# Expert tiles in groups of four, their narrow down halves on two row groups of TensorE

## What is computed

```python
x = x + xattn(layernorm(x), ctx, ctx, Wh, wg_w, wo_w, gn_gamma, gn_beta)
h = layernorm(x)
scores = softmax(h @ gate_w.T)                       # 64 experts
topk_w, topk_ids = top_k(scores, 6); topk_w /= sum(topk_w)
# for each expert e and each of its rows:
gu = h @ w_gate_up[e].T                              # 176 gate, 176 up
routed += comb[:, e] * ((silu(gu[:176]) * gu[176:]) @ w_down[e].T)
sgu = h @ ws_gate_up.T                               # shared: 352 gate, 352 up
out = x + routed + (silu(sg) * su) @ ws_down.T
```

## Time and profile before

| | |
|---|---|
| time, median of 3 runs | 310.27 us (308.89 to 312.10) |
| the profiled execution | 307.54 us, of which 305.7 us are the span |
| mean granted TensorE clock | 0.948 of full |
| PE, its weight loads, DVE, ACT, POOL busy | 87%, 75%, 49%, 41%, 58% |
| DMA | 89.08 MB, mean 291 GB/s |
| first product of tile 1, start of last scatter | 117.29 us, 290.47 us |

### The profile page before, as it was taken

How to read it: one execution, slowest core, us unless ns; L and a number is a source line. 1 busy time by engine, 2 the same in 40 slices (tenths; PEclk the granted TensorE clock), 3 DMA queues, 4 the chain that set the end, 5 groups by cost and what they waited for, 6 DMA issues and landing times.

```text
span 305.7 us, 6600 instructions
## 1 busy us (share of the span) xinstructions
PE 265.5 (87%) x1674; PEld 230.2 (75%) x1674; DVE 150.6 (49%) x696; ACT 125.3 (41%) x374; POOL 178.7 (58%) x155
## 2 busy tenths in 40 slices
PE   7998757698668986999999999999999999999830
PEld 4595435566455756999997999999999999999720
DVE  3835896489548672454423433333333333333446
ACT  2524433123122243555444555555555555555400
POOL 9201267457725670667888667676766666667620
PEclk9999998699959997999999999999999999999995
DMA  6999999999603363799999999999999999977598
GB/s 165 400 429 426 415 349 391 385 373 386 230 36 128 127 199 76 193 334 330 350 360 342 333 328 324 331 327 323 323 326 335 337 332 332 328 159 143 59 281 307
DMA packets 48071, 89.08 MB, mean 291 GB/s; under 512 B 6577, under 2 KB 32258, under 8 KB 47010
## 3 DMA queue, kind: packets, MB, share of 16 engines
q1 hardware_dynamic: 27154, 63.75, 57.8%
q0 software_dynamic: 12816, 17.12, 26.7%
q10 hardware_dynamic: 8064, 7.80, 7.5%
HBM read 58.11 MB, written 30.54 MB: 290 GB/s over the span
## 4 chain that ended last, share of the span: by engine, by line
PE 60%; issue 10%; DMA 10%; DVE 9%; ACT 4%; another core or an unknown queue 3%; POOL 2%; SPq 1%; POOLq 0%; ACTq 0%
PE PS L1188 26%; PE PS L1200 8%; PE PS L1201 8%; DMA acc<-PT,IDR 7%; PE PS L1057 4%; PE PS L1166 3%; PE PS L1140 2%; DMA CT<-in_ctxT 2%; PE PS L1020 2%; PE PS L1014 2%; DMA CT<-acc 1%; PE PS L1027 1%; PE PS L1035 1%; PE PS L1148 1%
## 5 line engine op out<-in xcount | busy, mean ns | idle before, releaser
L1188 PEld LDWEIGHTS PS<-XT,WA 128*128 128x128 f32 (+1 forms) x852 | 106.6, 188 | 7.8 <-ACT XNT L556 3.6
L1188 PE MATMUL PS<-XT,WA 128*128 128x128 f32 (+1 forms) x852 | 107.4, 276 | 3.8 <-ACT XNT L556 3.3
L492 POOL DMA_INDIRECT acc<-PT,IDR x52 | 81.0, 1558 | 37.4 <-ACT PT L660 16.4
L934 DVE TENSOR_TENSOR AC<-SG,PS 128x128 f32<-128x128 f32 x71 | 20.5, 288 | 99.7 <-ACT SG L628 72.5
L446 POOL DMA_INDIRECT x_slots<-HX,SLOT x36 | 35.5, 987 | 24.1 <-DVE SLOT L824 14.1
L660 ACT ACTIVATE PT<-PS,WT 128x256 f32<-128x256 f32 x70 | 33.2, 474 | 31.5 <-issue 18.7
L1200 PE MATMUL PS<-WA,AC 128*128 128x256 f32 x140 | 42.1, 383 | 0.6 <-issue 0.6
L1201 PE MATMUL PS<-WB,AC 128*128 128x256 f32 x140 | 41.6, 379 | 0.0
L492 POOL DMA_INDIRECT out_rows<-PT,IDR x18 | 28.1, 1562 | 18.9 <-ACT PT L660 12.3
L627 ACT ACTIVATE SG<-PS 128x128 f32<-128x128 f32 x71 | 19.7, 277 | 36.8 <-PE PS L1188 26.5
L549 ACT COPY XT<-PS 128x256 f32<-128x256 f32 x73 | 27.1, 372 | 18.5 <-PE PS L1057 10.4
(11 more groups left out here) (154 smaller groups left out, 317.3 us busy)
## 6 DMA issues: line engine op xcount, KB each, us to landing
WA<-in_wa SPq DMA_DIRECT2D x71, 496.0 KB
x_slots<-WA SPq DMA_DIRECT2D x1, 8704.0 KB, 28.6
VXG<-x_slots ACTq DMA_DIRECT2D x56, 136.0 KB
WB<-in_wb SPq DMA_DIRECT2D x71, 48.0 KB
acc<-ZERO SPq DMA_DIRECT2D x2, 1152.0 KB
VXG<-x_slots SPq DMA_DIRECT2D x8, 136.0 KB
CT<-in_ctxT SPq DMA_DIRECT2D x2, 512.0 KB, 6.2
X<-in_x SPq DMA_DIRECT2D x2, 512.0 KB, 6.4
```

The lines of the kernel that those rows point to most:

```text
L492: pool.indirect_dma_start(acc[j], bass.IndirectOffsetOnAxis(ap=IDR[:, u:u + 1], axis=0), YS[:, u % YR, :], None, compute_op=ALU.add).then_ ...
L934: v.tensor_tensor(AC[:, w % 2, 0, :], SG[:, w % 2, 0, :], PS[:, 4 + w % 2, 0:128], ALU.mult)
L1188: last = mm(PS[0:n, (4 if c == 2 else 2) + w % 2, c % 2 * 128:(c % 2 + 1) * 128], WA[:, base:base + n], XT[:, w % 2, k, :], start=(k == 0) ...
```

## The change

- Main tiles go in groups of four, the first four as two groups of two, on PE and ACT. Per group: gate and up and transposes for four tiles, then four wide halves, then four narrow halves, and one signal `s_d` for all four. ACT scales and stores the four results one behind the other after the group's four steps. Overflow tiles go singly.
- Narrow halves: activations of even tiles lie on partitions 0 to 47, of odd ones on 64 to 111, and so do the 48 rows of down in `WB`; the product has 48 rows instead of 128. Four results are held in two PSUM banks: even tiles in bank 6, odd ones in 7. `AC` and `WB` need no clearing.
- Blocks 6 and 7's shared products are computed transposed, features on partitions (12 products of 128 columns instead of 4 of 352), and DVE writes the product straight into `KEEP`: no turn and no copy of these two.
- The list is turned into a row by two small products on PE ahead of the transposes of tile 6, and copied by DVE (`list_row`); no DMA.
- The scatters into the accumulators get a bound (`bounds_check=N - 1`, no error beyond it).

```diff
+QUAD = 4
+LIST_W = 6
...
-        AC = sb("AC", [128, 2, 2, 128])
+        AC = sb("AC", [128, QUAD + 2, 128])
...
-        WB = sb("WB", [128, R * D])
+        WB = sb("WB", [128, R // 2 * D])
...
+        def narrow_weights(u):
+            return WB[UG * (u % 2):UG * (u % 2) + F2, u // 2 * D:(u // 2 + 1) * D]
+        def narrow_rows(w):
+            return AC[UG * (w % 2):UG * (w % 2) + F2, QUAD + w // 2 % 2, :]
+        def result(w):
+            return PS[:, 6 + w % 2, w // 2 % 2 * D:(w // 2 % 2 + 1) * D]
...
-            sp.wait_ge(s_wbz, 1)
...
             sp.wait_ge(s_list, 1)
-            sp.dma_start(lst_d, LST[:]).then_inc(s_lstd, 16)
             for t in range(4, XR):
                 x_first(t)
-            sp.wait_ge(s_lstd, 16)
-            sp.dma_start(LROW[:], lst_d.rearrange("(o t) c -> o (t c)", o=1)).then_inc(s_lrow, 16)
...
-                                        YS[:, u % YR, :], None, compute_op=ALU.add).then_inc(s_acc[j], 16)
+                                        YS[:, u % YR, :], None, compute_op=ALU.add,
+                                        bounds_check=N - 1, oob_is_err=False).then_inc(s_acc[j], 16)
...
@@ ACT
+            def group(i, u, n=QUAD):
+                for j in range(n):
+                    step(i, u + j)
+                for j in range(n):
+                    result_out(i, u + j)
...
-                ge(dve, s_d, t + (w - 1))
+                ge(dve, s_d, t + (w - QUAD + 1))
...
+                if isinstance(i, int) and t + w == LIST_W:
+                    pe.wait_ge(s_list, 1)
+                    for c in range(2):
+                        last = mm(PS[0:1, w % 2, 256 + c * 128:256 + (c + 1) * 128], LSF[:, c:c + 1], IDN, start=True, stop=True)
+                    last.then_inc(s_lturn, 1)
+                if isinstance(i, int) and t + w == LIST_W + 2:
+                    pe.wait_ge(s_lrow, 1)
...
+                            for c, n in enumerate(SC):
+                                at = g * SF + c * 128
+                                for k in range(KD):
+                                    last = mm(PS[0:n, GATE + g, c * 128:(c + 1) * 128], WSG[:, k, at:at + n],
+                                              HT[:, k, s * S:(s + 1) * S], start=(k == 0), stop=(k == KD - 1))
...
@@ PE
+            def wide(i, u, first):
+                pe.wait_ge(s_act, i * U + (u + 1))
+                mm(result(u), AC[:, u % QUAD, :], WA[:, u * WROW + KD * GUW:(u + 1) * WROW], start=first, stop=False,
+                   skip_group_check=not first)
+            def narrow(u, first):
+                return mm(result(u), narrow_rows(u), narrow_weights(u), start=False, stop=True, skip_group_check=not first)
+            def group(i, u, n=QUAD):
+                t = i * U
+                for j in range(n):
+                    gate_up(i, u + j + 1)
+                    rows(i, u + j + LOOK_R)
+                ge(pe, s_y, t + u)
+                for j in range(n):
+                    wide(i, u + j, j < 2)
+                for j in range(n):
+                    last = narrow(u + j, j < 2)
+                last.then_inc(s_d, n)
+            def late_step(i, u):
+                t = i * U
+                gate_up(i, u + 1)
+                rows(i, u + LOOK_R)
+                pe.wait_ge(s_y, t + (u - 1))
+                wide(i, u, True)
+                narrow(u, True).then_inc(s_d, 1)
...
             rows(0, 2)
-            turn_shared(B - 1)
-            pe.wait_ge(s_stc, B)
-            for u in range(U):
-                step(0, u)
+            pe.wait_ge(s_sact, B)
+            pe.wait_ge(s_stc, KEPT)
+            group(0, 0, 2)
+            group(0, 2, 2)
+            for u in range(QUAD, U, QUAD):
+                group(0, u)
```

More of the change, by code:

```diff
@@ L371, in load_late @@
                 load_next(i, u, e)
+            sp.wait_ge(s_lrow, 1)
             load_late(E // U, 0)
@@ L659, in finish_step @@
                 act.wait_ge(s_share, t + (u + 1))
[L660 removed]
+                nc.scalar.activation(YS[:, u % YR, :], result(u), ACT.Copy,
                                      scale=WT[:, u % 4:u % 4 + 1]).then_inc(s_y, 1)
             silu(0, 0)
[L664 removed]
             rows_in(0, 2)
[L666 to L667 removed]
+            group(0, 0, 2)
+            group(0, 2, 2)
+            for u in range(QUAD, U, QUAD):
+                group(0, u)
             with act.Fori(1, E // U - 1) as i:
[L669 to L672 removed]
+                for u in range(0, U, QUAD):
+                    group(i, u)
+            for u in range(0, U, QUAD):
+                group(E // U - 1, u)
             act.wait_ge(s_list, 1)
@@ L1215, in _ @@
             with pe.Fori(1, E // U - 1) as i:
-                for u in range(U):
-                    step(i, u)
-            for u in range(U):
-                step(E // U - 1, u)
-            late_tiles(pe, T, step)
+                for u in range(0, U, QUAD):
+                    group(i, u)
+            for u in range(0, U, QUAD):
+                group(E // U - 1, u)
+            late_tiles(pe, T, late_step)
             pe.wait_ge(s_xt2, T + LOOK_R)
```

86 lines of the change are left out of this document (44 added, 42 removed).

## The result

| | before | after |
|---|---|---|
| median of 20 runs each | 311.51 us | 313.74 us (310.37 to 315.13) |
| ratio | | **1.0122** (95% interval 1.0098 to 1.0146): slower |
| the profiled execution, its span | 307.54, 305.7 us | 315.12, 313.2 us |
| mean granted TensorE clock | 0.948 | 0.922 |
| first product of tile 1, tile 1 leaves PE | 117.29, 123.75 us | 122.36, 127.98 us |

The account below looks back on a forecast made before the run. PE was taken to bound the kernel, weights some 17 us ahead. Terms -6.1 + 1.4 - 1.4 + 0.4 + 2.1 - 1.0 = -4.6 us took the median from 310.27 to about 305.7; own range 301.5 to 308.5, with rivals 297 to 316.

Parts of the forecast that it names:

- tile follows tile on PE alone: Main and overflow tiles: PE sets the pace with nothing between tiles, 2.41 us each, 70 periods.
- Rival 3: Narrow halves: row groups do not overlap, a group pays only its switches; +5.6 us, 315.9 us; chance 0.13.
- Narrow halves, -6.1: Groups of four: five slots plus 0.12 us per switch, a gain of 0.41 us per group, 15 groups.
- rival 1: Narrow halves: full pairing and free switches; -12.4 us, 297.9 us; chance 0.18.
- rival 2: Narrow halves: overlap, but each switch at 0.24 us; -0.5 us, 309.8 us; chance 0.17.
- Overflow tiles, +1.4: Six overflow tiles have nothing to pair with but switch twice each: 6 x 0.24 us.
- Start, -1.4: Tiles 0 and 1, without block 7's turn and copy: leave PE at 122.4 us against 123.75.
- Transposed shared products, 0: Blocks 6 and 7: +0.28 us each stands against at most 0.55 from the dropped turn: nothing.
- List, +0.4: Tile 6: four extra PE passes of 128 columns cost 0.4 us; DVE's copy is hidden.
- ACT at a group's end, 0 with a bound of 4.5: Four results back to back leave margins of 0.15 to 0.3 us: nothing, or up to 0.3 per group.
- POOL at the end, +2.1: After the last group (end G), ten scatters and a gather: last scatter at G + 19.3 instead of 17.2 us.
- Padding rows, -1.0: Scatters' bound: padding rows need not be moved, easing DMA and the last landing; bounds 0 and -3 us.

Follow-up runs that it names:

- g2: f1 with the rows' weights `WT` eight deep instead of four; ratio 1.0057.
- g4: The change with shared products and list as before, gathers one per group, weights eight deep, tiles 60 on singly without row groups, bound kept; ratio 1.0035.
- e4: The change with groups of four kept but every narrow half on 112 of 128 rows, so no row groups; ratio 1.0303.
- f1: The change with shared products and list as before and no bound on the scatters: groups and row groups alone; ratio 1.0148.
- g1: f1 with POOL's eight gathers spread, one per group behind tiles 8 to 36; ratio 1.0064.
- r2: The changed kernel again, unchanged; ratio 1.0129.
- f2: The kernel before with only the bound on the scatters into the accumulators; ratio 0.9970.
- h4: g4 with the scatters of tiles 60 on bounded at row 0, so nearly none of their rows is written; ratio 0.9947.
- k1: The kernel before, no groups, with the bound, gathers one per four tiles, weights eight deep, late accumulators 0, 1, 2; ratio 0.9959.
- k2: h2 unchanged, taken again beside k1; ratio 0.9961.
- h2: g4 with tiles 56 on singly and late accumulators in the order 0, 1, 2; ratio 0.9880.
- e1: The change with the shared products of blocks 6 and 7 put back as before; ratio 1.0093.

## Why the prediction was wrong

The sum was off by 8.4 us (by the terms below, 8.9). What failed is the step from "tile follows tile on PE alone" to a sum in which waits of the other engines cost nothing: the gathers (3.0, not in the sum), DVE's wait for ACT at a group's end (1.5, put at nothing), and the start, which came out 2.4 us the other way. The list, the overflow tiles and the end were each 0.6 to 1.1 too low. The gain of the groups themselves was there. Rival 3 had a time near the measured one (+5.6) by a mechanism that the traces refute: the row groups do overlap.

**What bounds the kernel** was half seen. PE sets the pace of single tiles, with the earlier trace rows as evidence. But two more chains lay under it. A scatter on one accumulator lands 7.7 us after its issue and may be followed only then, some 8.1 us from one to the next: with four accumulators that leaves a group of 9.18 about 1 us, but three in turn, from tile 60 on, make 2.7 us a tile against PE's 2.41. And POOL has 1.86 us of its own per tile, 3.2 with a gather. The prediction priced the second only at the end, and left the first out of its sum. "On PE alone" was true of single tiles that come at 2.41 us; results in fours, and a pace a few per cent higher, use up the room.

**Narrow halves, -6.1: right in sum by luck, wrong in both terms.** The group's period is 9.18 (g2, g4), 0.47 under 9.65; forecast 0.41. But the passes pair fully (four slots, 0.86, which was rival 1's) and a switch costs 0.20 (nearly rival 2's 0.24), not five slots and 0.12; the two errors cancel. The argument that both passes of a product sit on the same rows, so that only one of them can pair with a neighbour's, was the step that failed. That changing the tiling mode drains TensorE (the Trainium skill, TensorEngine Tiling (Array Packing), Key Properties) agrees with the 0.19 to 0.20 us at each side.

**Overflow tiles, +1.4: mis-sized**, +2.5 (six tiles at 2.81 instead of 2.41, the first 2.96). The middle of 0 and 0.24 was taken for a switch; the row at 0.24 was the better guide.

**Start, -1.4: wrong sign**, +0.4 to +1.6 (five traces; e4 is the exception). The hole of ACT was taken to stay ahead of SiLU. It moved ahead of the tanh of block 7, where PE's gate and up of tile 0 stand behind it instead of beside it, and are slow as well (2.90 us). A stall of unknown cause can't be costed as if it were tied to the instruction that it precedes.

**Transposed shared products, 0**: part of the same. **List, +0.4: mis-sized**, 1.46: the products were counted (0.53), the way back over DVE was called hidden since DVE is half idle. It is idle, but in order: the copy stands behind two other instructions, and PE waits for it.

**ACT at a group's end, 0 with a bound of 4.5**: the bound holds, the nothing was wrong. Steady groups lose 0.05 in the change (second gate and up 1.38), 0.14 to 0.28 each in the five from 201.6 to 248.7 us, and deeper weights take that away (g2): 1.5 us in all.

**The term that is missing** is the gathers. They were not in the sum at all: 3.0 us in the change (groups of 9.86, 10.49, 9.83 and 9.56 where 9.18 is possible), 5.5 in f1, of which one group has 4. The prediction knew that POOL is handed bursts and looked for the effect only at the end; g1, which spreads the gathers, takes f1's long group away.

**POOL at the end, +2.1**: the burst is there, the size low: G + 20.8 and G + 21.2 (r2) for the last scatter, against G + 19.3; 2.5 to 2.9 us more behind PE than before. The first of the ten starts at G + 2.2, not G + 1.3, behind the landing of tile 57's scatter, a wait that the prediction named and left out of its sum.

**Padding rows, -1.0**: 0.997 (f2), which is 0.9 us, not resolved from nothing.

The corrected sum is -7.0 (15 groups by 0.47) + 2.5 + 1.0 (middle of the start) + 1.5 (list) + 1.5 (DVE's wait for ACT) + 3.0 (gathers) + 2.7 (end) - 0.9 = +4.3 us, against +3.8 measured. The same terms give f1, which has neither the turned list nor transposed products nor the bound, -7.0 + 2.5 + 1.8 + 5.5 + 2.2 = +5.0, against its 1.0148 (+4.6).

## What to carry to other kernels

Before taking 5% off the engine that sets the pace, write down the period of every chain beside it, also those of waits between transfers (issue, landing, next issue on the same target), and not only busy shares: POOL was 58% busy and still set the end. Handing work over in fours keeps every average and takes the slack out of every ring of buffers behind it, so look for all places where such a ring is already lent out, and for whatever else is queued on the engine that takes the burst. Compare traces between marks that lie behind the noisy stretch, and give a repaired version a control that has the repairs alone.

## What was not expected of the hardware

- Two float32 products on different row groups run together: eight passes of 256 columns in four slots of 0.216 us, with 0.20 us to enter and 0.19 to leave; one product costs 0.63 and two cost 0.63, so with the way back two are even with the whole array and four gain 0.47. The Trainium skill (TensorE: Matmul & The Clock Gate, Why this matters for your kernels) has products on distinct row groups run concurrently; this case's traces agree, for float32 too.
- DVE or ACT stood 2 to 10 us without a cause in the profile in all 18 traces up to h4 and in neither of k1 and k2. k2 is h2 to the letter, so the place of the code alone is not the cause; nor is the chip, as k1 and k2 carry the chip number of e1 to e4, whose traces have these stretches. What is the cause stays open.
- PE's clock follows: in the change, behind a wait of 3.85 us on PE, the granted clock was 0.56 from 120 to 125 us, between its two levels (1.2 and 2.4 GHz), and gate and up of tile 0 took 2.90 us instead of 1.33.
- A bound on the accumulating scatters left their instruction at 1.55 us, and took 2.9 MB off their queue (17.12 to 14.26 MB in f2).
